# Decoder layer on one core: in each pass of the cross-attention loop the next pass's scores are computed ahead of this pass's values

## The reference

```python
q = (norm(x) @ Wq).reshape(32, 64, 32, 128).transpose(0, 2, 1, 3)   # 32 heads of 128
k = (ctx @ Wk).reshape(32, 64, 8, 128).transpose(0, 2, 1, 3)        # 8 key-value heads
v = (ctx @ Wv).reshape(32, 64, 8, 128).transpose(0, 2, 1, 3)
q = q * cos + rotate_half(q) * sin
k = k * cos + rotate_half(k) * sin
k, v = repeat(k, 4, axis=1), repeat(v, 4, axis=1)
scores = einsum('bhqd,bhkd->bhqk', q, k) / sqrt(128)
scores = where(mask == 0, -1e9, scores)
x = x + einsum('bhqk,bhkd->bhqd', softmax(scores), v).transpose(0, 2, 1, 3).reshape(32, 64, 4096) @ Wo
```

## Time and profile before

| | us |
|---|---|
| median of 3 runs | 1466.87 (1465.68 to 1469.05) |
| the profiled execution | 1468.24 |
| its span | 1466.2 |
| PE busy in the span | 1403.5 (96%) |
| DVE busy | 1029.9 (70%) |
| POOL busy | 520.8 (36%) |
| ACT busy | 417.2 (28%) |

### The profile page before, as it was taken

One profiled execution on the slowest core, in us unless ns is written; L12 is line 12 of the kernel. 1 busy time (PEld: TensorE's weight loads), 2 busy tenths in 40 slices (PEclk: granted clock), 3 DMA queues, 4 the chain that ended last, 5 costly groups with the idle time before them and its releaser, 6 DMA issues.

```text
span 1466.2 us, 27911 instructions
## 1 busy us (share of the span) xinstructions
PE 1403.5 (96%) x11616; PEld 1160.9 (79%) x11616; DVE 1029.9 (70%) x1472; ACT 417.2 (28%) x710; POOL 520.8 (36%) x459
## 2 busy tenths in 40 slices
PE   7999999999995679999999999999999999999999
PEld 6788888788884568888888888888888888878787
DVE  3655553788887677777777776777877777778754
ACT  4211233655662321222222222222122122122321
POOL 4322220434431244344344344244344344342221
PEclk9999999999998789999999999999999999999999
DMA  8564320000000411111111011111011011003011
GB/s 246 187 194 165 115 87 1 16 10 17 10 2 28 131 44 37 37 50 39 30 58 30 29 58 37 32 49 44 30 44 44 29 44 44 30 15 106 7 58 58
DMA packets 79115, 84.08 MB, mean 57 GB/s; under 512 B 9824, under 2 KB 50928, under 8 KB 78736
## 3 DMA queue, kind: packets, MB, share of 16 engines
q1 hardware_dynamic: 68976, 63.42, 13.8%
q10 hardware_dynamic: 9216, 16.78, 3.5%
q0 software_dynamic: 800, 2.11, 0.5%
HBM read 59.22 MB, written 23.07 MB: 56 GB/s over the span
## 4 chain that ended last, share of the span: by engine, by line
PE 57%; DVE 6%; issue 2%; ACT 2%; POOL 1%; DMA 0%; ACTq 0%; SPq 0%; DVEq 0%
PE p_ps_q L75 4%; PE p_ps_q L77 4%; PE p_ps_q L76 4%; PE p_ps_s L1057 4%; PE p_ps_o L1097 4%; PE p_ps_o L1095 4%; PE p_ps_o L1096 4%; PE p_ps_y L1095 3%; PE p_ps_y L1096 3%; PE p_ps_y L1097 3%; PE p_ps_o L75 3%; PE p_ps_o L76 3%; PE p_ps_o L77 3%; PE p_ps_o L1082 3%; PE p_ps_s L1068 2%
## 5 line engine op out<-in xcount | busy, mean ns | idle before, releaser
L1416 POOL TENSOR_TENSOR p_q_rot<-p_q_rot,p_rb 128x512 f32<-128x512 f32 x128 | 166.4, 1300 | 346.5 <-DVE p_rb L164 346.5
L1195 ACT ACTIVATE p_o_hi<-p_ps_o 128x512 fp32r<-128x512 f32 x128 | 66.9, 601 | 244.3 <-PE p_ps_o L1082 244.3
L893 POOL TENSOR_TENSOR p_pn<-p_p,p_inv 128x512 f32<-128x512 f32 x64 | 66.2, 1065 | 162.5 <-DVE p_inv L817 159.9
L75 PE MATMUL p_ps_q<-p_xt_hi,p_wq_hi 128*128 128x512 f32 x256 | 108.5, 424 | 0.1
L1301 DVE TENSOR_TENSOR p_o_lo<-p_ps_o,p_o_hi 128x512 fp32r<-128x512 f32 x128 | 80.2, 684 | 38.2 <-ACT p_o_hi L1195 37.9
L1189 ACT ACTIVATE p_pt_hi<-p_ps_s 128x512 fp32r<-128x512 f32 x64 | 38.2, 599 | 238.1 <-PE p_ps_s L1068 238.0
L75 PE MATMUL p_ps_o<-p_xt_hi,p_wq_hi 128*128 128x512 f32 x256 | 103.8, 405 | 0.0
L77 PE MATMUL p_ps_q<-p_xt_hi,p_wq_lo 128*128 128x512 f32 x256 | 101.5, 396 | 0.0
L1095 PE MATMUL p_ps_y<-p_wo_hi,p_o_hi 128*128 128x512 f32 x256 | 100.2, 392 | 1.3 <-DVE p_o_lo L1301 1.3
L76 PE MATMUL p_ps_q<-p_xt_lo,p_wq_hi 128*128 128x512 f32 x256 | 100.7, 393 | 0.0
L76 PE MATMUL p_ps_o<-p_xt_lo,p_wq_hi 128*128 128x512 f32 x256 | 100.5, 392 | 0.0
(11 more groups left out here) (234 smaller groups left out, 3662.5 us busy)
## 6 DMA issues: line engine op xcount, KB each, us to landing
v_scratch<-p_v_out SPq DMA_DIRECT2D x32, 256.0 KB
k_scratch<-p_k_out SPq DMA_DIRECT2D x32, 256.0 KB, 2.1
p_raw<-in_wq SPq DMA_DIRECT2D x32, 256.0 KB, 3.1
p_k_t<-k_scratch ACTq DMA_DIRECT2D x32, 256.0 KB, 2.7
p_v_in<-v_scratch ACTq DMA_DIRECT2D x32, 256.0 KB, 2.9
p_raw<-in_wo SPq DMA_DIRECT2D x32, 256.0 KB, 2.6
x_sb<-in_x SPq DMA_DIRECT2D x16, 256.0 KB, 3.0
out<-p_y SPq DMA_DIRECT2D x16, 256.0 KB, 2.0
```

Source lines behind the costliest of these rows:

```text
L75: nc.tensor.matmul(out, lh, rh, start=(c == 0), stop=False)
L893: nc.gpsimd.tensor_tensor(pn[:, u * PB:(u + 1) * PB, :, :].rearrange("p b j k -> p j b k"), part, scale.unsqueeze(3).broadcast_to([P, HALF ...
L1195: nc.scalar.activation(o_hi[:, half * UT:(half + 1) * UT, :, r, :], ps_o[2 * half + r][:, :].rearrange("p (t h q) -> p t h q", t=UT, h=H), ...
L1416: nc.gpsimd.tensor_tensor(q_rot[:, h, :], q_rot[:, h, :], rb[:, :], ALU.add).then_inc(q_added, 1)
```

## The change

On PE, in every pass, `scores(it + 1)` moves from behind the two `mix` to ahead of them. On DVE the function `shift` is cut in two: `limit` (the two minima) moves ahead of `outputs_lo(it, 0)`, and the rest, still called `shift`, stands between `outputs_lo(it, 0)` and `outputs_lo(it, 1)`. ACT, POOL and the DMA queues keep their order. No instruction is added or taken away.

```diff
             for it in range(LAST - 1):
+                scores(it + 1)
                 mix(it, 0)
                 mix(it, 1)
-                scores(it + 1)
                 queries(it + 2, 0)
                 output(it, 0)
...
+            scores(LAST)
             mix(LAST - 1, 0)
             mix(LAST - 1, 1)
-            scores(LAST)
             output(LAST - 1, 0)
...
-            def shift(it):
+            def limit(it):
...
+            def shift(it):
+
+                if it >= ITS:
+                    return
                 need(dve, s_bound, 2 * (it + 1))
...
             rotate(1, 0)
+            limit(0)
             shift(0)
...
                 if it > 0:
                     add(it - 1, 3)
+                limit(it + 1)
                 outputs_lo(it, 0)
+                shift(it + 1)
                 outputs_lo(it, 1)
-                shift(it + 1)
                 rotate(it + 2, 0)
...
             add(LAST - 2, 3)
+            limit(LAST)
             outputs_lo(LAST - 1, 0)
+            shift(LAST)
             outputs_lo(LAST - 1, 1)
-            shift(LAST)
```

## The result

The changed kernel takes 1483.7 us (median of 4 runs, 1482.0 to 1485.67), the kernel before beside it 1467.96: ratio 1.011 (95% interval 1.0091 to 1.0129). It is slower by 15.7 us, as forecast (1482.1). The profiled execution took 1482.0, its span 1480.2, against 1468.24 and 1466.2.

The account below looks back on a forecast made before the run. PE, busy 96% of the span, was taken to bound the kernel. Terms 0.6 + 10.4 + 1.0 + 1.1 + 0.65 + 1.45 = 15.2 us on 1466.87 gave 1482.1, range 1473 to 1488.

Parts of the forecast that it names:

- the first passes 4 to 24: Six first passes of a group: late weight splits make each 29.1 against 27.36, 1.7 more, 10.4 us in all.
- pass 28: First pass of the last group: late weight splits make it 29.1 against 28.13, 1.0 us more.
- pass 29: Statistics (0.69) are added, so the transposes' load comes at 15.27 against 14.67: 0.65 us more.
- pass 30: End of the loop: no queries cover output, which waits 1.35 for its low part; DVE's picks come later; 1.45 us.
- ordinary passes: Subtraction waits for POOL's values' low part, the transposes' slack shrinks to nearly nothing: 0.05 in 22 passes, 1.1 us.
- start of the loop: The first scores need both low parts of the probabilities where mix needed only the first: 0.6 us.
- The output weights: First passes: ACT's weight splits stand behind outputs that wait for mix; POOL's low parts start 2.02 later, PE 1.5 late.
- The port: First passes: DVE's subtraction and POOL's splits take turns, so PE is 2.45 late, not 1.5.
- rival 1: First passes: POOL keeps the port through all four splits and the subtraction waits; 1485 to 1493 us, chance 0.16.
- Rival 3: First passes: the subtraction fits between splits at no cost to them; 1476 us, 1473 with cheap shape changes; chance 0.13.
- Rival 2: Ordinary passes: softmax 0.2 later than worked out, 22 passes lose 0.2 to 0.25 each; 1487 us, chance 0.08.

Follow-up runs that it names:

- weights ahead: Changed kernel with ACT making the output weights' high parts ahead of the outputs' high parts in first passes of a group: 1466.84 us, ratio 0.9986.
- PE's half only: Kernel before with only PE's scores moved ahead of the two mix, DVE's order kept: 1501.21 us, ratio 1.0223.
- shift behind both low parts: Changed kernel with maximum and subtraction behind both outputs' low parts in the seven first passes only: 1478.02 us, ratio 1.006.
- subtraction from PSUM: Changed kernel with row maximum and subtraction reading the scores in PSUM, mask left out of the softmax: 1475.44 us, ratio 1.0046.

## Why the prediction was right

**The sum by its terms.** From the passes' starts in the two profiles, with what was forecast in brackets: the first passes 4 to 24 without pass 20 1.60 to 1.67 each, 8.2 together, and pass 20 another 3.2, so 11.4 (10.4); pass 28 29.01 in place of 28.13, 0.9 (1.0); pass 29 27.31 in place of 26.62, 0.7 (0.65); pass 30 31.03 in place of 29.59, 1.4 (1.45); 22 ordinary passes, pass 0 among them, -0.7 in all (+1.1); start of the loop 538.90 in place of 538.59, 0.3 (0.6). That makes 14.0, and the spans differ by 14.0; 15.2 was forecast. The 0.3 at the start is the forecast 0.6 and a chance of this execution: the last low part of the probabilities, which ended at 539.08 before, ended at 538.76 here, before the first instruction that the change moves, and PE began 0.14 behind it where it had begun 0.49 ahead of it. (POOL's last rotation for pass 1, for which the scores wait as well, ended 0.03 behind that low part; the prediction did not name it.)

**The output weights.** Right, and shown: with the splits freed from the values (weights ahead) the changed kernel goes from 15 us over before to 2.8 under.

**The port.** Right, and shown from two sides: with the subtraction out of the splits' way the first passes fall from 29.0 to 28.15, with one SBUF operand fewer to 28.05. The choice between the forecast and rival 1 was also right: the subtraction waited for one split, took the port, and the next split took 2.26 us in place of 1.30. Rival 3's case, a run of splits that loses nothing, is what these two variants bring about.

**Ordinary passes.** The mechanism was right, the slack ran out to the last 0.1 (the load waits 0.18), but the term of 1.1 was mis-sized: nothing was lost, and 0.03 a pass was gained. The new sequence of matmul shapes, which the prediction kept at up to 0.1 a pass, is not what gains: in pass 13 the queries start at 3.65 behind the pass's start (3.64 before), and the last output matmul lies 0.32 ahead of the next burst in both kernels. Pass 13 has gained 0.01 by the first transposes and 0.04 by the second (17.84 against 17.88); why is open. Rival 2, which needed 0.2 more, did not happen.

**What the prediction had not got.** A fall of PE's clock behind the new waits, 1.6 us in pass 20. It was in no term and in no rival. Without it the profile's difference would have been 12.4 against the 15.2 forecast. Of these 2.8 us, 1.8 are the ordinary passes, 0.7 the first passes, whose seven delays came out 0.1 smaller each, and 0.3 the chance at the loop's start. With it, 14.0: the near match rests partly on terms that were too large covering one that was missing.

Luck has a part in the last digits as well. Single executions of one kernel differ by 2 to 4 us, and the two profiles of the changed kernel show where: their spans are 1480.2 and 1483.5, and the burst of pass 0 starts at 538.90 in the first and at 542.13 in the one taken once more.

```profile
538.90 3.68 PE L1057 MATMUL p_ps_s<-p_k_t,p_q_rot 128*64 128x64 f32 x64 [3.99 <-POOL p_q_rot L1424]
...
542.13 3.68 PE L1057 MATMUL p_ps_s<-p_k_t,p_q_rot 128*64 128x64 f32 x64 [3.84 <-POOL p_q_rot L1424]
```

So 3.2 of the 3.3 us lie ahead of the loop, and the clock behind the new waits is not their cause: the falls in the loop are the same in both. What differs ahead of the loop is open. The 1.6 us between forecast and median are within that scatter.

Two small slips of the prediction decide nothing: by its own terms rival 1's sum begins at 17 and not at 18, and the chances of all cases but the last two add up to 0.92, not 0.91.

## What to carry to other kernels

On an engine's order, look past the step that is moved to what the other engines hang behind it: here the scores' 2 us moved the values, ACT's copies, POOL's splits and PE's weights in a row. The cheap cure was one engine further back, in the order of ACT, and it served the old kernel better than the new one. Before two-operand SBUF work on DVE is put elsewhere, see what POOL runs there: beside a dense run on POOL both are held up, and the loss lands where someone waits for the run's last instruction.

## What the runs showed of the hardware

The clock: behind three waits of 0.42, 1.69 and 0.72 us that end 2.2 and 1.25 us apart, PE's granted clock fell in some passes and not in others of the same shape, in 7 of 35 over the five profiles that have these waits. Each of the seven falls began 10.9 to 11.1 us into its pass, just behind the end of the third wait (10.80). In pass 20 of the changed kernel the three waits are those of pass 12, and then (matmuls of 512 columns, start to start 0.43 us in place of 0.24):

```profile
1095.06 0.63 PE L75 MATMUL p_ps_o<-p_xt_hi,p_wq_hi 128*128 128x512 f32 x1
1095.49 0.63 PE L76 MATMUL p_ps_o<-p_xt_lo,p_wq_hi 128*128 128x512 f32 x1
...
1098.31 0.40 PE L75 MATMUL p_ps_o<-p_xt_hi,p_wq_hi 128*128 128x512 f32 x1
1098.55 0.39 PE L76 MATMUL p_ps_o<-p_xt_lo,p_wq_hi 128*128 128x512 f32 x1
```

The granted clock over 1094 to 1096 us was 0.55, that is mostly the 1.2 GHz level, and 1.00 again from 1098. Each fall cost 1.6 us. The transfers are not what tells the passes apart: the same stretch of pass 12 (876.34 to 878.34) has a DMA share of 0.77 and a clock of 1.00, where pass 20 has 0.82 and 0.55. In the three variants whose waits were 0.4, 0.7 and 0.7 us (PE's half only, shift behind both low parts, subtraction from PSUM) it did not happen in any of the 21 profiled first passes. The Trainium skill (TensorE: Matmul & The Clock Gate, "What's actually happening") says that the window of the activity monitor is free-running and does not reset when a kernel starts. The traces fit that, since the same waits are followed by a fall in one pass and by none in another; no run here tests it by itself.

What the clock costs at the loop's start varies too: pass 0 took 29.21 us at a mean granted clock of 0.90 in the changed kernel's profile, and 28.09 at 0.94 in that of the shift behind both low parts, with the same work on PE. Such a 1.1 us between two single profiles is not the edit's.

The port: a DVE subtraction of two SBUF operands that arrived during a POOL run ended 1.08 us behind the POOL instruction that it met, and the POOL instruction after it 1.13 behind the subtraction; neither was slowed when DVE's other operand lay in PSUM.
